# Graph layer kernel: finding each node's edges by samples, and the key sums taken as a column of the value product

## The chip, the cores and the metric

The kernel runs on one core of one Trainium2 chip. The metric is the device time of one execution, in microseconds (us), as the median of several runs. A profile is one further execution, recorded by the hardware profiler; its span is the time from its first to its last recorded instruction. The engines are PE (TensorE; its weight loads are listed apart, as PEld), DVE (VectorE), ACT (ScalarE), POOL (GpSimd) and SP, which issues most transfers.

## The reference

x has 1250 rows (nodes) of 1024 values. Everything below works on xn, the layer norm of x.

```
# graph part: 40,000 edges (src, dst, type), sorted by dst, 8 types
u = xn @ root + bias
for r in range(8):
    u += mean over the edges of type r into each node of xn[src] @ weight[r]
z = concat(u, xn) @ w_gate + b_gate
h = tanh(u) * z + xn * (1 - z)
# linear attention, 16 heads of 64
q, k = elu(xn@Wq)+1, elu(xn@Wk)+1;  v = xn@Wv;  g = sigmoid(xn@Wg + bg)
kv = k^T v (per head);  k_sum = sum of k over the nodes
out = (q*scale @ kv) / clip(q . k_sum) * g @ Wo
x = x + h + out
# gates, one step from a zero state
x = x + sigmoid(o) * tanh(sigmoid(i) * tanh(c)),  each of layernorm(x) @ W
```

## The kernel before, in words

**Dense products.** The 1250 nodes are ten tiles of 128 (the last has 98). PE computes 38 stages in a fixed order, each one weight matrix half (1024 by 512) against all ten tiles (stages `G_` and `Q_` use 12 units of 416 or 418 columns). One tile of one stage is a unit, numbered q from 0. Each product is made of three: high part by high part, and the two mixed terms, so a unit is 8 (k) times 3 = 24 matmuls. Units 0 to 159 are the `Y_` stages (xn by the eight relation weights), 160 to 179 `R_`, then `V_` (180 to 189 and 200 to 209), `K_` (190 to 199 and 210 to 219), `X_`, `G_`, `Q_`, `O_` and the gates. The order of every engine is written out by hand: each engine runs a loop over q and over k = 0 to 7, and small pieces of other work are put in at chosen (q, k).

**Weights.** A stage's weights come in four granules. SP loads a granule (`load_w`), ACT casts the high part (`hi_w`, L936) and DVE subtracts for the low part (`lo_w`, L1080) in units 1, 3, 5 and 7 of the stage before. `load_w` of granule n+2 waits until the low part of granule n is made, since the raw buffer has two places. SP's queue is in order: behind a waiting `load_w` stand the stores of finished units (`store_unit`, L536). ACT empties a PSUM tile into `res`, which has three places (`evict`, L961), and waits for the store of the unit three before (`free_res`). PE may start unit q when unit q-3 is evicted.

**Edge tables.** While the `Y_` stages run, the edges are sorted into per-node tables. DVE splits dst into tile and place (`edge_cells`, at the start, between `ln_x(1)` and `lo_w(4)`). In units 20 to 40 the edges per node and relation are counted: DVE writes one-hot tiles of 8 edges per partition (`count_step`, L1133) and PE multiplies them (L792), 40 steps of 8 matmuls. The counts give in-degrees, keys and reciprocals (`in_degrees`, unit 41), PE turns them into first positions (`run_starts`, unit 42), and POOL fetches for each node two rows of 64 edge codes (`read_run`, 20 indirect DMAs). DVE marks which codes belong to each node (`run_inside`, `run_keys`, `run_half`, units 43 to 46). In units 48 to 57, at each unit twice, DVE ranks a tile of nodes by degree (`rank_tile`, L1214 and L1215) and takes the 40 highest codes of a tile (`top_of`, L1225 and L1227). `tables` (units 59 and 61) makes row numbers and weights; POOL scatters the tables to memory (`send_rows`), SP loads them back (`load_edges`, L573, units 63 and 69: it waits for all ten scatters of a half). `columns_over` (DVE, unit 75) checks the table widths, `any_bad` (PE, unit 76, k = 2) sums the flags and `which_path` sets a flag `meta`: if it is 1, a slow general path loops over all edges.

**Sums.** From unit 82 POOL gathers rows of the `Y_` results (L1626) and DVE adds them up (`add_edges`, L1299), some 2.3 steps a unit, up to the `G_` stages.

**Keys and values.** Beside each `K_` unit PE adds one node tile to kv (`kv_tile`, k = 6 of the unit after): for each of four blocks of 128 columns one fp32 matmul of the key tile against the value tile (L821, PSUM bank `misc`) and one of the same key tile against two columns of ones (L824, bank `tp`), so 8 matmuls. The values come back from memory by `load_v`, one DMA a tile in pieces of 2048 bytes, into two places; the load for tile t waits until `kv_tile` t-2 is done.

Of the kernel before, what the change touches and what calls it, by code (L numbers as in the profile page):

```python
# [5 lines left out]
F32 = mybir.dt.float32  # L6
# [22 lines left out]
CB = 8  # L29
COUNTS = EC // CB  # L30
B = R * T
NOBODY = 1 << 20
# [4 lines left out]

RUN = 64
RUN_ROWS = E // RUN + 2
# [134 lines left out]
def build(nc, x, src, dst, edge_type, weight, root, bias, w_gate, b_gate, Wq, Wk, Wv, Wg, bg, Wo,  # L174
          W_iT, b_i, W_oT, b_o, W_cT, b_c, out):
    with ExitStack() as ctx:
# [19 lines left out]
        code_d = dram("code_d", [RUN_ROWS, RUN])  # L196
        key_d = dram("key_d", [2, T * 128])
# [23 lines left out]
        inv = put("inv", [128, B])  # L221
# [8 lines left out]
        ones2 = put("ones2", [128, 2])  # L230
# [19 lines left out]
        cells = at(e_at + 5120, "cells", [128, 2, EC], I32)  # L250
        bucket = at(e_at + 7680, "bucket", [128, EC])
        node = at(e_at + 8960, "node", [128, EC])
        b80 = at(e_at + 10240, "b80", [128, EC])
        code = at(e_at + 11520, "code", [128, EC])
        tmp = at(e_at + 12800, "tmp", [128, EC])
        falls = at(e_at + 14080, "falls", [128, EC])
        tail = at(e_at + 15360, "tail", [128, 1])
        assert e_at + 15392 <= end
        oh_node = at(wx_at, "oh_node", [128, 2, CB, 128], BF16)
        oh_bucket = at(wx_at + 4096, "oh_bucket", [128, 2, CB, B], BF16)  # L260
        before = at(wx_at + 6656, "before", [128, 128])
        assert wx_at + 7168 <= e_at


        nodes = at(M + 44448, "nodes", [128, T], I32)
        turned_key = at(M + 44512, "turned_key", [128, T])
        cnt = at(M + 44576, "cnt", [128, 2, T])
        deg = at(M + 44672, "deg", [128, T])
        key = at(M + 44736, "key", [128, 2, T])
        rank = at(M + 44832, "rank", [128, 2, T])  # L270
        slot = at(M + 44928, "slot", [128, 2, T], I32)
        first = at(M + 45024, "first", [128, T])
        run_row = at(M + 45088, "run_row", [128, 2, T], I32)
        run_off = at(M + 45184, "run_off", [128, T])
        most = at(M + 45248, "most", [128, T])
        assert M + 45312 <= end and M + 40960 + up(16 * COLS) + 32 * T <= M + 44448
        runs = at(M, "runs", [128, T, 2 * RUN])
        held = at(M + 5120, "held", [128, 2, T, 2 * RUN])
        dist = at(M + 15360, "dist", [128, T, 2 * RUN])
        inside = at(M + 20480, "inside", [128, T, 2 * RUN])  # L280
        made = at(M + 25600, "made", [128, T, 2 * RUN])
# [4 lines left out]
        p_at = M + 15360  # L286
        whole = at(p_at, "whole", [128, T, WIDE], I32)
        source = at(p_at + 1600, "source", [128, T, WIDE])
        relation = at(p_at + 3200, "relation", [128, T, WIDE])
        weigh = at(p_at + 4800, "weigh", [128, T, WIDE])  # L290
        part_w = at(p_at + 6400, "part_w", [128, T, WIDE])
        assert M + 33920 + 80 * ROW <= M + 40960


        vld = at(M, "vld", [128, 2, H])
        U = [at(M + 4096, "U0", [128, D]), at(M + 12288, "U1", [128, D])]
        kv = at(M + 8192, "kv", [128, PAIRS, 128])
        odd = at(M + 16384, "odd", [128, D])
        ring = at(M + 20480, "ring", [128, RING, D])
        edge = at(M + 40960, "edge", [128, 2, COLS, 2], I32)  # L300
        whose = at(M + 40960 + up(16 * COLS), "whose", [128, 2, T, 2], I32)
        assert M + 40960 + up(16 * COLS) + 32 * T <= end and RING * 4096 == 20480


        x_raw = at(M + 16384, "x_raw", [128, D], F32R)
        x_big = at(M + 20480, "x_big", [128, D], F32R)
        x_oh = at(M + 24576, "x_oh", [128, 128], F32R)
        x_edge = at(M + 25088, "x_edge", [128, 3], I32)
        x_part = at(M + 25120, "x_part", [128, 2], I32)
        x_sum = at(M + 25152, "x_sum", [128, 3])  # L310
        x_idx = at(M + 25184, "x_idx", [128, 3], I32)
        x_inv = at(M + 25216, "x_inv", [128, 1])
# [4 lines left out]
        o0 = at(M + 12288, "o0", [128, 4, N])  # L317
        o1 = at(M + 32288, "o1", [128, 2, 4, GROUPS[0][1]])
        assert M + 32288 + 32 * GROUPS[0][1] <= end
# [7 lines left out]
        lnb = at(M + 40960, "lnb", [128, 2, H])  # L327
# [8 lines left out]
        def turned_rows(w):  # L336
# [14 lines left out]
        edges_in, cells_made, edges_made, tail_made, codes_st, bg_in = (  # L351
            sem(n) for n in ("edges_in", "cells_made", "edges_made", "tail_made", "codes_st", "bg_in"))
        sum_const, cnt_oh, cnt_mm, inv_done, inv_st, deg_made, run_mm, run_made, runs_in = (
            sem(n) for n in ("sum_const", "cnt_oh", "cnt_mm", "inv_done", "inv_st", "deg_made", "run_mm", "run_made",
                             "runs_in"))
# [135 lines left out]
        def _(sp):  # L491
# [202 lines left out]
            for q in range(UNITS + 1):  # L694
# [13 lines left out]
                if q < UNITS:  # L708
# [10 lines left out]
                    if q == 43:  # L719
                        store_keys()  # L720
                    if q == 47:
                        load_keys()
# [1046 lines left out]
```

## Time and profile before

| what | value |
|---|---|
| median of 3 runs | 2356.18 us (2354.4 to 2358.92) |
| the profiled execution, its own time | 2352.61 us |
| its span | 2350.9 us |
| PE busy | 2241.8 us (95%) |
| PE weight loads busy | 1826.0 us (78%) |
| DVE busy | 1310.4 us (56%) |
| POOL busy | 710.6 us (30%) |
| ACT busy | 438.7 us (19%) |
| mean granted PE clock | 0.983 |

Busy time is the time in which an engine executes; where it is below the span, the views of waits and windows say where it stood still. Matmuls are pipelined, so one matmul's listed duration (0.39 us) is longer than the distance to the next.

### The profile page before, as it was taken

What the parts mean: (1) busy time and instruction counts of PE and PEld (TensorE: products, weight loads), DVE (VectorE), ACT (ScalarE), POOL (GpSimd) and SP (SyncE); (2) the same over time, 40 slices, a digit from 0 to 9 for tenths busy, and PEclk for the clock granted to TensorE, in tenths of its full rate; (3) what the DMA queues carried; (4) which work ended last, traced back from release to release, by engine and by line L of the source; (5) the groups of instructions that cost most, each with busy time, mean ns of one, the idle gap of its engine ahead of it and who ended that gap; (6) DMA issues with size and microseconds to landing.
All of it is one profiled execution on the core that took longest, in us unless ns stands there. A gap on an engine that the chain in (4) does not pass through costs nothing.

```text
span 2350.9 us, 26012 instructions
## 1 busy us (share of the span) xinstructions
PE 2241.8 (95%) x10294; PEld 1826.0 (78%) x10294; DVE 1310.4 (56%) x1695; ACT 438.7 (19%) x623; POOL 710.6 (30%) x586
## 2 busy tenths in 40 slices
PE   5999997399999999999999999999999799999999
PEld 4877775288888888888888888899887687887787
DVE  6446549931666666666645556765782347424233
ACT  2111111011111111110121210122231213322121
POOL 3200030041555556644534334561111254000000
PEclk9999998699999999999999999999999999999999
DMA  6442230143778888875767768883016865213112
GB/s 213 176 118 76 71 102 30 57 116 118 257 246 291 287 318 287 294 271 173 278 224 236 257 222 287 280 301 135 27 46 237 327 235 179 69 57 107 49 37 74
DMA packets 186039, 420.98 MB, mean 179 GB/s; under 512 B 34309, under 2 KB 41078, under 8 KB 185916
## 3 DMA queue, kind: packets, MB, share of 16 engines
q1 hardware_dynamic: 122716, 233.42, 28.9%
q0 software_dynamic: 63200, 185.89, 23.7%
q8 instruction: 81, 1.33, 0.2%
q14 instruction: 42, 0.34, 0.1%
HBM read 356.62 MB, written 103.70 MB: 196 GB/s over the span
## 4 chain that ended last, share of the span: by engine, by line
PE 81%; DVE 7%; issue 5%; DMA 4%; POOL 2%; SPq 0%; ACT 0%; POOLq 0%; DVEq 0%; ACTq 0%
PE acc L926 72%; PE acc L921 5%; DVE top_codes L1225 1%; DMA th_d<-tu 1%; DVE rank L1215 1%; DVE held L1227 1%; PE misc L821 1%; PE tp L779 1%; POOL o L1731 1%; DVE Wlo L1080 1%; DVE above L1214 1%; POOL runs L1606 1%; DMA uio<-u_d 1%; PE misc L792 1%; DMA tx<-xn_d 0%
## 5 line engine op out<-in xcount | busy, mean ns | idle before, releaser
L926 PE MATMUL acc<-Whi,aThi 128*128 128x512 f32 (+1 forms) x2720 | 1088.0, 400 | 71.5 <-DVE Wlo L1080 34.5
L926 PE MATMUL acc<-Whi,aTlo 128*128 128x512 f32 (+1 forms) x2720 | 1076.1, 396 | 0.0
L926 PE MATMUL acc<-Wlo,aThi 128*128 128x512 f32 (+1 forms) x2720 | 1074.0, 395 | 0.0
L926 PEld LDWEIGHTS acc<-Whi,aThi 128*128 128x128 f32 (+1 forms) x2720 | 507.8, 187 | 197.6 <-DVE Wlo L1080 37.4
L1626 POOL DMA_INDIRECT ring<-y_d,edge x390 | 480.1, 1231 | 515.0 <-DVE U L1299 173.4
L926 PEld LDWEIGHTS acc<-Whi,aTlo 128*128 128x128 f32 (+1 forms) x2720 | 507.3, 187 | 128.0
L926 PEld LDWEIGHTS acc<-Wlo,aThi 128*128 128x128 f32 (+1 forms) x2720 | 508.9, 187 | 122.8 <-issue 0.2
L1080 DVE TENSOR_TENSOR Wlo<-Wraw,Whi 128x1024 fp32r<-128x1024 f32 x149 | 186.4, 1253 | 266.4 <-ACT Whi L936 265.7
L961 ACT COPY res<-acc 128x512 f32<-128x512 f32 (+1 forms) x180 | 105.6, 587 | 931.4 <-PE acc L926 788.9
L1299 DVE SCALAR_TENSOR_TENSOR U<-ring,edge,U 128x1024 f32<-128x1024 f32 x180 | 230.3, 1279 | 33.1 <-DMA ring<-y_d,edge 32.8
L1299 DVE SCALAR_TENSOR_TENSOR odd<-ring,edge,odd 128x1024 f32<-128x1024 f32 x170 | 217.7, 1281 | 47.7 <-DMA ring<-y_d,edge 46.9
L936 ACT CAST Whi<-Wraw 128x1024 fp32r<-128x1024 f32 x149 | 155.4, 1047 | 197.2 <-PE acc L926 53.8
L1382 DVE TENSOR_TENSOR res<-acc,bias_sb 128x512 f32<-128x512 f32 x80 | 55.3, 692 | 187.4 <-PE acc L926 116.8
L921 PE MATMUL acc<-aThi,Whi 128*128 128x416 f32 (+1 forms) x384 | 142.3, 371 | 0.0
L921 PE MATMUL acc<-aTlo,Whi 128*128 128x416 f32 (+1 forms) x384 | 135.1, 352 | 0.0
L921 PE MATMUL acc<-aThi,Wlo 128*128 128x416 f32 (+1 forms) x384 | 134.8, 351 | 0.0
L1606 POOL DMA_INDIRECT runs<-code_d,run_row x20 | 21.1, 1055 | 182.6 <-DVE run_row L1171 176.8
L921 PEld LDWEIGHTS acc<-aThi,Whi 128*128 128x128 f32 x384 | 72.2, 188 | 4.7 <-issue 3.7
L921 PEld LDWEIGHTS acc<-aTlo,Whi 128*128 128x128 f32 x384 | 72.3, 188 | 4.4 <-issue 3.7
L1085 DVE TENSOR_TENSOR aTlo<-tp,aThi 128x1024 fp32r<-128x1024 f32 (+1 forms) x30 | 35.9, 1196 | 71.0 <-ACT aThi L940 71.0
L1361 DVE SCALAR_TENSOR_TENSOR res<-acc,res 128x512 f32<-128x512 f32 (+3 forms) x44 | 26.6, 604 | 85.3 <-ACT res L974 85.3
L921 PEld LDWEIGHTS acc<-aThi,Wlo 128*128 128x128 f32 x384 | 72.2, 188 | 0.7
(182 smaller groups left out, 1272.8 us busy)
## 6 DMA issues: line engine op xcount, KB each, us to landing
y_d<-res SPq DMA_DIRECT2D x144, 256.0 KB
Wraw<-in_L_gnn_weight SPq DMA_DIRECT2D x61, 512.0 KB, 4.8
Wraw<-in_L_gnn_w_gate SPq DMA_DIRECT2D x16, 512.0 KB, 6.4
ring<-y_d,edge POOLq DMA_INDIRECT x390, 6.5
xr<-in_x SPq DMA_DIRECT2D x9, 512.0 KB, 3.8
xn_d<-xnb SPq DMA_DIRECT2D x9, 512.0 KB, 3.0
xs_d<-xr SPq DMA_DIRECT2D x9, 512.0 KB, 3.8
ur_d<-res SPq DMA_DIRECT2D x18, 256.0 KB
```

Of the source, the lines that this page charges most:

```text
L779: tr = nc.tensor.transpose(tp[:, k // 4, (k % 4) * 128:(k % 4) * 128 + w], parts(k), ident[0:w, 0:w])
L921: mm = nc.tensor.matmul(to, a[:, s % 2, k, cols], b[:, k, c0:c0 + w], start=start, stop=stop)
L926: mm = nc.tensor.matmul(to, a[:, k, rows(i)], b[:, s % 2, k, :], start=start, stop=stop)
L936: nc.scalar.copy(granule(Whi, n), raw(n)).then_inc(w_hi, 1)
L961: nc.scalar.copy(res[0:width(i), q % 3, :], acc[0:width(i), q % 3, :]).then_inc(evac_a, 1)
L1080: nc.vector.tensor_tensor(granule(Wlo, n), raw(n), granule(Whi, n).bitcast(F32), ALU.subtract).then_inc(w_lo, 1)
L1085: nc.vector.tensor_tensor(aTlo[:, :, rows(t)], turned_rows(width(t)), aThi[:, :, rows(t)].bitcast(F32), ALU.subtract).then_inc(done, 1)
L1299: nc.vector.scalar_tensor_tensor(to, g, scale, to, ALU.mult, ALU.add).then_inc(u_acc, 1)
L1361: nc.vector.scalar_tensor_tensor(a, p, 0.0, a, ALU.max, ALU.add).then_inc(evac_v, 1)
L1382: nc.vector.tensor_tensor(to, p, bias_sb[0:w, n % 2, :], ALU.add).then_inc(evac_v, 1)
L1606: pool.indirect_dma_start(runs[:, t, i * RUN:(i + 1) * RUN], None, code_d, bass.IndirectOffsetOnAxis(ap=run_row[:, i, t:t + 1], axis=0), b ...
L1626: pool.indirect_dma_start(ring[:, j % RING, :], None, a, bass.IndirectOffsetOnAxis(ap=index, axis=0), bounds_check=top - 1, oob_is_err=Fal ...
```

## The change

1. **Counting goes.** `edge_cells`, the 40 `count_step`s (DVE and PE), `in_degrees` and `run_starts` are removed. `edge_codes` on POOL makes code = dst * 10000 + type * 1250 + src and a copy of every 64th code, the samples (625). They are stored to memory and read back to all 128 partitions (`load_samples`, SP, unit 21). DVE counts for each tile of nodes how many samples are below the node's first code (`count_below`, units 23 to 27), which gives the first row of 64 codes (`run_places`, unit 28).
2. **Marking moves and changes.** After the 20 indirect reads, DVE subtracts the node's code and compares with the half's limits (`run_codes`, `run_half`, `run_keys`, `hold_half`, units 36 to 39). The in-degrees are sums of these marks.
3. **Ranking and taking the highest codes are spread.** `top_of` and `rank_tile` run in two of every three units, once each, in units 41 to 72. Reciprocals of the counts per relation are made from the table itself (`tables_weights`, unit after `tables`). `tables` runs in units 58 and 73, `tables_weights` in 59 and 74, `load_edges` in 61 and 76, `columns_over` in 78, `any_bad` at unit 79 and `which_path` at unit 80.
4. **Keys and values.** The value tile is held as four blocks of 130 columns, 128 values and two ones, so that four matmuls of 130 columns give kv and the key sums; `load_v` writes it in pieces of 512 bytes.
5. The general path counts for itself; it does not run on these inputs unless a flag is set. The store of `inv` (unit 63) goes.

```diff
-                if k in (1, 5) and 0 <= 2 * q + k // 5 - 41 < COUNTS:
-                    count_step(2 * q + k // 5 - 41)
-                if q == 42 and k == 2:
-                    run_starts()
-                if q == 76 and k == 2:
+                if q == 79 and k == 2:
                     any_bad()
...
                 for m in range(4):
-                    nc.tensor.matmul(misc[:, m * 128:(m + 1) * 128], rows_k[:, m * 128:(m + 1) * 128],
-                                     vld[0:w, t % 2, m * 128:(m + 1) * 128], start=(t == 0 and m == 0),
-                                     stop=(t == T - 1), skip_group_check=True)
-                    mm = nc.tensor.matmul(tp[:, 0, 2 * m:2 * m + 2], rows_k[:, m * 128:(m + 1) * 128], ones2[0:w, :],
-                                          start=(t == 0 and m == 0), stop=(t == T - 1), skip_group_check=True)
+                    to = (misc[:, :] if m < 2 else tp[:, 0, :])[:, m % 2 * 130:m % 2 * 130 + 130]
+                    mm = nc.tensor.matmul(to, rows_k[:, m * 128:(m + 1) * 128], vld[0:w, t % 2, m, :],
+                                          start=(t == 0 and m % 2 == 0), stop=(t == T - 1), skip_group_check=True)
...
+            def load_samples():
+                sp.wait_ge(codes_st, 48)
+                for i in range(2):
+                    sp.wait_ge(xn_st[i], 16 * (T // 2))
+                    sp.wait_ge(xs_st[i], 16 * (T // 2))
+                sp.dma_start(sample_row[:, :], sample_d.rearrange("(o n) -> o n", o=1).to_broadcast([128, SAMPLES])
+                             ).then_inc(samples_in, 16)
...
+            def count_below(t):
+                if t == 0:
+                    dve.wait_ge(samples_in, 16)
+                    dve.wait_ge(const, 3)
+                chain(nc.vector.tensor_scalar(below[:, :], sample_row[:, :], node_code[:, t:t + 1], None, ALU.is_lt))
+                chain(nc.vector.tensor_reduce(below_n[:, t:t + 1], below[:, :], AX.X, ALU.add))
...
+            def run_half(h):
+                lowest, beyond = float(h * HALF_R * N), float((h + 1) * HALF_R * N)
+                chain(nc.vector.tensor_scalar(within[:, h, :, :], runs[:, :, :], lowest, None, ALU.is_ge))
+                chain(nc.vector.scalar_tensor_tensor(within[:, h, :, :], runs[:, :, :], beyond, within[:, h, :, :],
+                                                     ALU.is_lt, ALU.mult))
+                step.inc(nc.vector.tensor_reduce(bad[:, 1 + h:2 + h], within[:, h, :, 2 * RUN - 1], AX.X, ALU.max))
+                chain(nc.vector.tensor_reduce(cnt[:, h, :], within[:, h, :, :], AX.X, ALU.add))
...
+            def tables_weights(h):
+                for r in range(HALF_R):
+                    step.inc(nc.vector.scalar_tensor_tensor(of_r[:, r, :, :], relation[:, :, :], float(r),
+                                                            weigh[:, :, :], ALU.is_equal, ALU.mult))
+                step.wait(dve)
+                for r in range(HALF_R):
+                    step.inc(nc.vector.tensor_reduce(inv[:, r, :], of_r[:, r, :, :], AX.X, ALU.add))
...
+                for r in range(HALF_R):
+                    step.inc(nc.vector.tensor_tensor(of_r[:, r, :, :], of_r[:, r, :, :],
+                                                     inv[:, r, :].unsqueeze(2).to_broadcast([128, T, WIDE]), ALU.mult))
...
-                    if k in (1, 5) and 0 <= 2 * q + k // 5 - 40 < COUNTS:
-                        count_step(2 * q + k // 5 - 40)
...
-                    if 48 <= q < 48 + T and k in (1, 5):
-                        rank_tile((q - 48) // 5, 2 * ((q - 48) % 5) + k // 5)
...
-                    if 48 <= q < 48 + T and k in (2, 6):
-                        top_of((q - 48) // 5, 2 * ((q - 48) % 5) + k // 5)
...
+                    if k == 1 and 41 <= q < 71 and (q - 41) % 3 < 2:
+                        top_of((q - 41) // 15, 2 * ((q - 41) % 15 // 3) + (q - 41) % 3)
+                    if k == 5 and 43 <= q < 73 and (q - 43) % 3 < 2:
+                        rank_tile((q - 43) // 15, 2 * ((q - 43) % 15 // 3) + (q - 43) % 3)
+                    if q in (58, 73) and k == 1:
+                        ranks_whole((q - 58) // 15)
+                    if q in (58, 73) and k == 2:
+                        tables((q - 58) // 15)
+                    if q in (59, 74) and k == 1:
+                        tables_weights((q - 59) // 15)
+                    if q == 78 and k == 5:
+                        columns_over()
+                    if q == 80 and k == 2:
+                        which_path()
```

## Rows read from the trace of the kernel before

**Rows 1.** Page, costliest groups: count, busy and mean ns, idle before and its releaser

```profile
L1080 DVE TENSOR_TENSOR Wlo<-Wraw,Whi 128x1024 fp32r<-128x1024 f32 x149 | 186.4, 1253 | 266.4 <-ACT Whi L936 265.7
L961 ACT COPY res<-acc 128x512 f32<-128x512 f32 (+1 forms) x180 | 105.6, 587 | 931.4 <-PE acc L926 788.9
...
L936 ACT CAST Whi<-Wraw 128x1024 fp32r<-128x1024 f32 x149 | 155.4, 1047 | 197.2 <-PE acc L926 53.8
```

**Rows 2.** Windows: busy us (instructions) of PE, PEld, DVE, ACT, POOL; clock; DMA

```profile
345.00:463.00 118.00, 62.22 (x240) 47.69 (x240) 104.86 (x291) 9.94 (x15) 0.00 (x0) 0.78 0.16 53
463.00:551.00 88.00, 87.85 (x372) 70.60 (x373) 31.25 (x66) 15.93 (x23) 24.70 (x21) 0.98 0.38 115
551.00:1195.00 644.00, 644.00 (x2793) 515.76 (x2792) 388.19 (x340) 100.68 (x142) 336.60 (x274) 1.00 0.76 259
```

**Rows 3.** Waits of the whole span: us in total, times, longest

```profile
ACT res L961 <- DMA y_d<-res: 142.4, 10, 32.1
...
PE acc L926 <- DVE Wlo L1080: 34.5, 6, 20.8
...
PE acc L926 <- ACT res L961: 27.3, 2, 16.8
...
PE misc L792 <- DVE oh_bucket L1133: 3.3, 1, 3.3
```

**Rows 4.** Waits of SP's queue in the stretch 340 to 470 us

```profile
SPq L497 <- DVE Wlo L1080: 104.2, 4, 37.2
```

**Rows 5.** Timeline of DVE from 351 us: start, duration, instruction

```profile
351.19 0.89 DVE L1214 TENSOR_SCALAR above<-keyrow,key 128x1280 f32<-128x1280 f32 x1 [5.94 <-DMA keyrow<-key_d]
352.12 1.49 DVE L1215 TENSOR_REDUCE rank<-above 128x1 f32<-128x1280 f32 x1
...
356.84 0.89 DVE L1214 TENSOR_SCALAR above<-keyrow,key 128x1280 f32<-128x1280 f32 x1
```

**Rows 6.** Chain that ended last, in order of time: start, us, what

```profile
174.40 2.87 PE acc L926 x12
177.57 2.87 PE acc L926 x12
...
551.28 641.81 PE acc L926 x2772
```

**Rows 7.** Timeline of DVE and of PE before the first counting step

```profile
156.72 1.23 DVE L1080 TENSOR_TENSOR Wlo<-Wraw,Whi 128x1024 fp32r<-128x1024 f32 x1 [1.12 <-ACT Whi L936]
...
159.88 0.38 PE L792 MATMUL misc<-oh_bucket,oh_node 125*128 125x80 bf16 x3 [3.26 <-DVE oh_bucket L1133]
```

**Rows 8.** Timeline of PE's weight loads inside one kv_tile

```profile
1215.26 0.30 PEld L821 LDWEIGHTS misc<-vld,res 128*128 128x128 f32 x2
1215.48 0.30 PEld L824 LDWEIGHTS tp<-ones,res 128*128 128x128 f32 x2
1215.70 0.30 PEld L821 LDWEIGHTS misc<-vld,res 128*128 128x128 f32 x2
```

**Rows 9.** Timeline of DVE at the start of the kernel

```profile
21.93 0.32 DVE L1118 TENSOR_SCALAR cells<-raw_edges 125x320 int32<-125x320 int32 x1
...
23.93 1.35 DVE L1080 TENSOR_TENSOR Wlo<-wx,Whi 128x1024 fp32r<-128x1024 f32 x1
```

**Rows 10.** Timeline of DVE, POOL and SP around the first half's tables

```profile
468.73 0.36 DVE L1234 CAST whole<-top_codes 128x400 int32<-128x400 f32 x1
...
472.44 0.57 DVE L1249 SCALAR_TENSOR_TENSOR weigh<-relation,inv 128x400 f32<-128x400 f32 x1
...
478.31 1.02 POOL L1613 DMA_INDIRECT slot_d<-table,slot  x1 [151.87 <-DVEq L1259]
...
490.15 0.97 POOL L1613 DMA_INDIRECT slot_d<-table,slot  x1 [0.30 <-issue]
...
493.50 4.81 SPq L573 DMA_DIRECT2D edge<-slot_d  x10
```

**Rows 11.** DMA issues in 460 to 620 us: count, size, median us to landing

```profile
whose<-slot_d SPq DMA_DIRECT2D x2, 10.0 KB, 2.3
```

**Rows 12.** Tile vld: the DMA's time to landing, min, median, max

```profile
DMA to landing us min/median/max: 2.5/4.0/6.5
```

More of the change, by code:

```diff
@@ L271, in build @@
[L271 to L274, printed above, removed]
+        code = at(e_at + 5120, "code", [128, EC])
+        tmp = at(e_at + 6400, "tmp", [128, EC])
+        falls = at(e_at + 7680, "falls", [128, EC])
+        tail = at(e_at + 8960, "tail", [128, 1])
+        samples = at(e_at + 8992, "samples", [128, EC // RUN])
+        assert e_at + 9024 <= end
@@ L786, in turn_x @@
                 turn_rows(lambda k: xnb[0:width(t), t % 2, k * 128:(k + 1) * 128], width(t)).then_inc(x_turned, 1)
[L788 to L803 removed]
             def any_bad():
+                pe.wait_ge(const, 3)
                 pe.wait_ge(bad_made, 1)
@@ L884, in general_sums @@
                 with pe.If(general > 0):
+                    with pe.Fori(0, EC) as c:
+                        pe.wait_ge(xc_oh, c * 2 + 2)
+                        nc.tensor.matmul(agg[:, 0, 0:B], x_node[0:EP, :], x_bucket[0:EP, :], start=True, stop=True
+                                         ).then_inc(xc_mm, 1)
                     with pe.Fori(0, T * EC) as i:
@@ new lines, in run_places @@
+            def run_places():
+                chain(nc.vector.tensor_scalar(most[:, :], below_n[:, :], 1.0, 1.0, ALU.max, ALU.subtract))
+                nc.vector.tensor_copy(run_row[:, 0, :], most[:, :]).then_inc(run_made, 1)
+                nc.vector.tensor_copy(run_row[:, 1, :], below_n[:, :]).then_inc(run_made, 1)
+                dve.wait_ge(run_made, 2)
+                chain(nc.vector.tensor_scalar(run_row[:, 1, :], most[:, :], 1.0, None, ALU.add))
+                dve.sem_inc(run_made, 1)
@@ new lines, in across, with everywhere, run_codes @@
+            def across(a):
+                return a.unsqueeze(2).to_broadcast([128, T, 2 * RUN])
+            def everywhere(a):
+                return a.unsqueeze(1).to_broadcast([128, T, 2 * RUN])
+            def run_codes():
+                dve.wait_ge(runs_in, 16 * 2 * T)
+                chain(nc.vector.tensor_tensor(runs[:, :, :], runs[:, :, :], across(node_code[:, :]), ALU.subtract))
+            def run_half(h):
[5 more added lines that the diff above has]
+                chain(nc.vector.tensor_reduce(cnt[:, h, :], within[:, h, :, :], AX.X, ALU.add))
@@ L1193, in run_keys @@
[L1193 to L1207 removed]
+                dve.wait_ge(place_const, 2)
@@ new lines, in run_keys, with hold_half @@
+                chain(nc.vector.scalar_tensor_tensor(runs[:, :, :], runs[:, :, :], float(2 * RUN),
+                                                     everywhere(odd_places[:, :]), ALU.mult, ALU.add))
+            def hold_half(h):
+                chain(nc.vector.tensor_tensor(held[:, h, :, :], within[:, h, :, :], runs[:, :, :], ALU.mult))
+                chain(nc.vector.tensor_tensor(held[:, h, :, :], held[:, h, :, :], everywhere(next_places[:, :]),
+                                              ALU.subtract))
@@ L1545, in _ @@
-                    if q == 75 and k == 5:
+                    if q == 17 and k == 6:
+                        edge_order()
+                    if 23 <= q < 28 and k in (2, 6):
+                        count_below(2 * (q - 23) + k // 6)
+                    if q == 28 and k == 2:
+                        run_places()
+                    if q == 36 and k == 2:
+                        run_codes()
+                    if q in (36, 37) and k == 6:
+                        run_half(q - 36)
+                    if q == 38 and k == 2:
+                        run_keys()
@@ new lines, in _ @@
+                    if q in (38, 39) and k == 6:
+                        hold_half(q - 38)
+                    if k == 1 and 41 <= q < 71 and (q - 41) % 3 < 2:
[4 more added lines that the diff above has]
+                        ranks_whole((q - 58) // 15)
```

350 lines of the change are left out of this document (147 added, 203 removed).

## The prediction

> **What bounds the kernel now.** I read the page's groups first, then a table of windows, the waits, and the timelines of the places that the change touches. PE is the bound, but not everywhere. From 551.28 us on, 2772 matmuls take 641.81 us without a gap [rows 6]: 0.2315 us each, so a unit of 24 takes 5.56 us, and in the window 551 to 1195 PE stands still nowhere [rows 2]. A microsecond taken from DVE there is worth nothing. The stretch before it is different: in 345 to 463 us PE runs 240 matmuls in 118 us at a mean clock of 0.78, while DVE is busy 104.9 us of the 118 [rows 2].
>
> The waits say how DVE holds PE. One `rank_tile` and one `top_of` take 356.84 - 351.19 = 5.65 us [rows 5], and two of each are written into each unit, so 11.3 us of DVE work per 5.56 us of PE work. The low parts of the weights stand in the same queue and come late. SP's queue waits 104.2 us for them at `load_w` [rows 4], the stores behind it come late, ACT waits 142.4 us for stores before it may evict [rows 3], and PE waits 27.3 us for evictions and 34.5 us for the low parts [rows 3]. So this stretch is bound by DVE, through SP's queue.
>
> **The change, part by part.** The sum is made against the profiled execution, 2352.6 us (span 2350.9 and 1.7 around it), which is 3.6 us under the median of the runs.
>
> *The DVE-bound stretch.* From 345.0 to 551.28 us PE does 240 + 372 = 612 matmuls [rows 2]. At 0.2315 us they are 141.7 us, the stretch is 206.3 us: 64.6 us are lost, in waits and in the slow restarts behind them. After the change a period of three units (16.7 us) holds two `rank_tile`s and two `top_of`s, 11.3 us, and 1.2 subtractions of 1.25 us [rows 1], together 12.8 us or 77%. In the crowded spot around unit 59 (`tables`, two `top_of`s, a `rank_tile` or two and `tables_weights` between the subtractions of units 57 and 61) I add up: lateness 1.5 us before, then 4.1 (tables, as 468.73 to 472.44 [rows 10] and one added comparison), 2.4 (a `rank_tile`, 0.89 + 1.49 [rows 5]), 3.2 (a `top_of`, the rest of the 5.65), 8.9, 2.4 and 3.2, in all 25.7 us in DVE's queue before the subtraction of unit 61, where the four units leave 20.9 beside it; the subtraction of unit 61 is some 5 us late, that of 63 some 6.6, 67 is on time again. A granule is needed only in the next stage, two to ten units on, so PE does not wait for these. The 8.9 us of `tables_weights` are 11 passes over 400 columns at 0.5 to 0.58 us [rows 10], four reductions taken at the same price, and 0.9 for small ones (an estimate). Earlier, `count_below` is at most ten times 0.89 + 1.49 us [rows 5] in five units (27.8 us), and `run_codes` to `hold_half` are nine passes over 1280 columns and two reductions, at most 1.49 us each, about 17 us in the 22 us of units 36 to 39, where no subtraction is due after unit 37. The 20 indirect reads start in unit 28 and take 26 us at the 1.3 us pace of the scatters ((490.15 - 478.31)/9 [rows 10]); they are in by unit 33 and DVE asks at 36. I take the full 64.6 us; the lower bound is 50 (rival B and more of the kind).
>
> *Counting steps.* With one step in every 12 matmuls the pitch is 177.57 - 174.40 = 3.17 us [rows 6]; 12 matmuls alone are 2.78. A step costs 0.39, 40 cost 15.7 us. The first also made PE wait 3.26 us for its one-hot tile [rows 7]; without it PE waits for the subtraction that ends at 156.72 + 1.23 = 157.95, so 1.9 us earlier than 159.88. With less slow restart I take 2.9 us (1.5 to 4). `run_starts` is two narrow matmuls, 0.4 us.
>
> *New waits at the tables.* `tables` for the second half follows the subtraction of unit 71, `tables_weights` that of unit 73. A subtraction ends 2.9 us into its unit (evict 0.59, cast 1.05, subtract 1.25 behind PE's last matmul [rows 1]), so with 8.9 us the tables are ready 0.7 us into unit 75. The first scatter starts 0.9 later, ten take 490.15 - 478.31 + 0.97 = 12.8 us, SP goes on 493.50 - 491.12 = 2.4 us after that [rows 10]: start of unit 78. Its ten loads take 4.8 us, the last one 0.5 and 2.3 to land [rows 10, 11]: 2 us into unit 79. DVE needs 0.8 us for four small operations (an estimate), so the flag is made 2.8 us into unit 79, and `any_bad` stands on PE at k = 2, 1.4 us into it. PE waits 1.4 us there, where before it waited for nothing (range 0 to 5). In the meantime SP is held from unit 75 to 79, and store 75 goes out 5.3 us into unit 78; eviction 78, due at the start of unit 79, comes some 2 to 3 us late, and PE asks for it only at unit 81. For the first half the same count gives: tables ready 1 us into unit 61, SP free and store 60 out by the start of unit 65, landed 2.7 us into it, eviction 63 done 3.3 us into it, needed at 66: 2.2 us to spare. That is the thinnest cover of this change. If the scatters or the loads take longer by a half, 8 us, PE waits 6 us there.
>
> *Keys and values.* The weight loads of a `kv_tile` come in doubles (an fp32 matmul is shown twice), and follow at 0.22 us for wide and narrow alike [rows 8], 0.11 per pass: eight matmuls are 1.78 us. Four stay. If a pass is bound by its weight load, a tile costs 0.89; if the narrow passes were cheaper and the wide ones dearer than the mean by an eighth, 0.125 each, it costs 1.0. I take 0.94: saving 20 times 0.84 = 16.8 us (15.6 to 17.8). All of it is PE time in a stretch with no gap, so it counts in full. The V loads are in four pieces where one was; they land in 4.0 us (at most 6.5) [rows 12], and have two units with a `kv_tile`, 13 us. Six copies to SBUF instead of three happen between K stages and are covered by DVE's free time.
>
> The Trainium skill, TensorE: Matmul & The Clock Gate, Back-to-back issue gap, gives a sustained distance of about 81 ns per matmul of 128 columns, weight load included. By it the eight passes that stay would be 0.65 us, the saving 22.6 us and the sum 6 us lower. The trace does not agree: the same passes stand 0.11 us apart.
>
> *The start.* `edge_cells` sits in DVE's queue from 21.93 to 23.93 [rows 9], in front of subtractions that PE and SP's next loads wait for. 2.0 us go (0 to 3). The check of the order moves to unit 17, where DVE waits anyway. POOL's codes start before DVE is done and run beside it.
>
> The sum: 64.6 + 15.7 + 2.9 + 0.4 - 1.4 + 16.8 + 2.0 = 101.0 us, so 2251.6 us for the profiled execution, and 2255 us at the median of runs.
>
> **The rivals.** *B: the tables' transfers hold PE.* The mechanism above with longer scatters or loads: SP stands at `load_edges`, no store leaves, ACT can't evict. For it: this is just the chain that stopped PE before [rows 3, 4], and the cover is 2.2 us. Against it: at 463 to 551 us the same scatters and loads ran with an SP stop of the same kind, and PE lost next to nothing (87.85 of 88 us) [rows 2]. Two stops of 5 us with a slow restart each: 2268 us. *C: DVE stays late.* If the DVE steps between subtractions take a half longer than summed, 19 us per 16.7, each of ten periods loses 2.5 us, and with slow restarts half of the lost time stays, 32 us: 2287 us. Against it: the durations are measured. *D: the sums slip.* The K units are 0.84 us shorter, so the additions, tied to units, have 17 us less; the last could hold the first attention unit by 5 us: 2260. DVE is busy 388 of 644 us beside the sums [rows 2], which speaks against it. *E, on the other side: V loads come late.* If a load in 512-byte pieces takes so long that `kv_tile` waits, each of 20 tiles pays. The room is 13 us and the gain to be eaten 101/20 = 5 us a tile, so it decides from 18 us to landing, four and a half times the median of 4.0 [rows 12]; at 20 us the time is 2356 + 40 = 2396. *F: it doesn't do what it says:* if the samples placed a node's codes wrongly, a flag would send the kernel down the general path, 3200 passes with three gathers of at least a microsecond each [rows 10], 10,000 us more. An average node has 32 edges in 128 codes read, so I see no reason.
>
> **How the numbers follow.** Forecast 0.66 (2247 to 2263), B 0.15, C 0.06, D 0.05, a gain larger than summed (below 2247, all terms at their upper bound: 2246) 0.04, E and F 0.03, no change 0.01. The range goes from 2244 to 2275, which takes in B and D. What a measurement of this kernel can tell from no change is about 0.2%, 5 us. Faster 0.96, same 0.01, slower 0.03.
>
> **What the profile will show.** PE in units 41 to 75 without gaps, clock 1.00; no wait of SP at `load_w` over 10 us; pitch of 24 matmuls and a `kv_tile` 6.5 us where it was 7.33 (5.56 + 1.78); one wait of PE for `any_bad` near unit 79; PE's first products of unit 20 some 2 us earlier. Wrong if PE stands at units 64 to 68 or 79 to 81 for more than 3 us each, if a 130-column pass is slower than 0.13 us, or if DVE's queue is over 90% busy between units 41 and 75.

## The result

The changed kernel takes 2249.88 us at the median (2248.53 to 2253.43), the kernel before 2355.78 us on the same chip: a ratio of 0.9551 with an interval of 0.9534 to 0.9568. The forecast was 2255 us, in a range of 2244 to 2275. The profiled execution took 2253.43 us with a span of 2251.6 us; the span of before was 2350.9 us. Run once more, later, the ratio was 0.9561 (0.9548 to 0.9574) and the span of the profile 2249.5 us.

The windows of the changed kernel, columns as in [rows 2]:

```profile
290.00:380.00 90.00, 90.00 (x390) 71.83 (x390) 69.93 (x181) 15.08 (x22) 0.00 (x0) 1.00 0.24 81
380.00:470.00 90.00, 90.00 (x391) 72.40 (x390) 63.59 (x150) 15.98 (x24) 18.80 (x18) 1.00 0.30 95
490.00:1108.30 618.30, 618.30 (x2673) 495.08 (x2673) 384.54 (x337) 97.28 (x137) 334.11 (x274) 1.00 0.79 267
1110.00:1287.00 177.00, 177.00 (x844) 145.14 (x843) 104.41 (x103) 41.49 (x61) 80.69 (x67) 1.00 0.78 258
```

Read the two first lines against the first of [rows 2]. Where 240 matmuls took 118 us at a clock of 0.78, PE now does 781 in 180 us, 0.23 us each, at the full clock. DVE is busy 78% and then 71% of the time, where it was 89%. Its work is mostly spread and only a little smaller: over the whole execution it is busy 1250.4 us and was 1310.4. At the crowded spot around unit 59, from 360 to 405 us, it is still busy 42.5 of 45 us, and PE loses nothing there.

Waits of the changed kernel, lines cut from the list: first two in the whole span, then all but the last of SP's queue from 140 to 490 us (total, times, longest):

```profile
ACT res L960 <- DMA y_d<-res: 21.3, 3, 11.1
...
PE tp L795 <- DMA uio<-u_d: 13.0, 2, 9.3
```

```profile
SPq L534 <- ACT res L960: 206.3, 53, 5.9
SPq L495 <- DVE Wlo L1079: 58.0, 24, 7.4
SPq L582 <- DMA slot_d<-table,slot: 33.5, 2, 20.7
```

The chain that held PE has gone link by link. SP's wait for the low parts had single pieces of up to 37.2 us [rows 4] and has none over 7.4 us, in a longer stretch; ACT's wait for stores fell from 142.4 to 21.3 us; PE's waits for evictions, 27.3 us [rows 3], are not in the list any more.

The chain that ended last, in order of time:

```profile
483.19 625.14 PE acc L925 x2700
1109.22 5.55 PE acc L925 x24
1115.67 5.55 PE acc L925 x24
...
1287.28 106.96 PE acc L925 x462
1394.24 104.63 PE acc L920 x552
```

Its joints date the gain. The series of 2700 matmuls that ends at the first K unit begins at 483.19 us; in [rows 6] the same matmul stands 72 into the 2772, at 551.28 + 16.68 = 567.96 us. So 84.8 us are won by unit 79. The start of the x462 piece, behind the K stages, stood at 1389.64 us in the chain of before: 102.4 us are won there, so the K stages gave 17.6. From there on nothing more is won, and 99.3 us are left at the end: PE waits 13.0 us for `uio` where it waited 9.9. That last loss is scatter between executions: in the repeated profile of the same kernel the wait was 9.9 us again, and the span 101.4 us under that of before.

### The profile page after: what moved, and what is told of

It is laid out like the page before. It is cut to its first block, busy times and chain, and to the rows that moved or that the text cites. A ratio compares the mean times of both kernels' runs of the same rounds, so it can differ in the third digit from the quotient of the medians.

```text
span 2251.6 us, 25006 instructions
## 1 busy us (share of the span) xinstructions
PE 2200.0 (98%) x9810; PEld 1796.0 (80%) x9810; DVE 1250.4 (56%) x1647; ACT 439.0 (19%) x623; POOL 715.0 (32%) x589
## 4 chain that ended last, share of the span: by engine, by line
PE 68%; issue 5%; DMA 3%; POOL 1%; DVE 1%; SPq 1%; ACT 0%; POOLq 0%; DVEq 0%; ACTq 0%
PE acc L925 61%; PE acc L920 5%; DMA th_d<-tu 1%; POOL o L1745 1%; DMA uio<-u_d 1%; PE tp L795 1%; DMA tx<-xn_d 1%; PE tp L823 0%; PE misc L823 0%; POOL tu L1749 0%; DMA o<-g_d 0%; POOL slot_d L1626 0%; SPq L582 0%; DVE aTlo L1084 0%; DVE x_scale L1474 0%
## 5 line engine op out<-in xcount | busy, mean ns | idle before, releaser
L925 PE MATMUL acc<-Whi,aThi 128*128 128x512 f32 (+1 forms) x2720 | 1080.7, 397 | 15.9 <-DVE aTlo L1084 10.3
L1626 POOL DMA_INDIRECT slot_d<-table,slot x20 | 21.8, 1089 | 227.3 <-DVEq L1239 221.8
L1745 POOL TENSOR_TENSOR o<-o,rden 128x416 f32<-128x416 f32 (+1 forms) x24 | 24.7, 1029 | 143.3 <-DVE rden L1421 143.3
```

Source lines behind the costliest of these rows:

```text
L925: mm = nc.tensor.matmul(to, a[:, k, rows(i)], b[:, s % 2, k, :], start=start, stop=stop)
L1626: pool.indirect_dma_start(slot_d[h], bass.IndirectOffsetOnAxis(ap=slot[:, h, t:t + 1], axis=0), table[:, h, t, :], None).then_inc(sent[h], 16)
L1745: nc.gpsimd.tensor_tensor(o, o, rden[:, a % 2, 0:w], ALU.mult).then_inc(shared_out, 1)
```

## The experiments

Twelve kernels ran in three groups of four, each group on a chip of its own. "Against the changed kernel" means the median less 0.9551 times the median of the kernel before on that chip, or less that of a named run on the same chip.

**Ranking packed again.** Two rankings and two top steps per unit in units 48 to 57, all else as changed.

```diff
-                    if k == 1 and 41 <= q < 71 and (q - 41) % 3 < 2:
-                        top_of(...)
-                    if k == 5 and 43 <= q < 73 and (q - 43) % 3 < 2:
-                        rank_tile(...)
+                    if 48 <= q < 48 + T and k in (1, 5):
+                        rank_tile((q - 48) // 5, 2 * ((q - 48) % 5) + k // 5)
+                    if 48 <= q < 48 + T and k in (2, 6):
+                        top_of((q - 48) // 5, 2 * ((q - 48) % 5) + k // 5)
```

> The changed kernel with rank_tile and top_of packed as before, twice a unit in units 48 to 57, nothing else undone. My theory (DVE's queue, packed, held PE through late low parts, SP's queue and late stores): the 64.6 us come back, 2250 + 65 = 2315 us (2300 to 2325), PE idle of some 55 us and a granted clock under 0.85 in that stretch, SP's queue at load_w waiting some 100 us. Rival (the counting and its waits made the stretch slow, spreading is worth little): within 5 us of 2250.

2309.84 us, ratio 0.9775 (0.9757 to 0.9792): 54 us against the changed kernel. Windows from 380 to 440 us:

```profile
380.00:400.00 20.00, 11.37 (x36) 7.88 (x36) 18.59 (x58) 2.02 (x3) 0.00 (x0) 0.76 0.11 41
400.00:420.00 20.00, 2.92 (x6) 1.82 (x6) 18.79 (x49) 1.17 (x2) 0.00 (x0) 0.50 0.17 52
420.00:440.00 20.00, 14.97 (x54) 12.01 (x55) 18.86 (x52) 2.13 (x3) 0.00 (x0) 0.74 0.20 63
```

DVE is full, and PE does 6 matmuls in the middle one, where some 86 fit: the old bound is back with the old order alone, and so are its links: from 320 to 490 us SP's queue waits 91.0 us for low parts at `load_w`, ACT 102.5 us for stores, and PE 27.5 us for low parts and 15.9 for evictions. It costs a sixth less than the 64.6 us of before.

**Ranking spread and nothing else.** The kernel before, with one pair of steps per unit in units 48 to 67 and the tables, loads and checks moved behind them.

```diff
-                    if 48 <= q < 48 + T and k in (1, 5):
-                        rank_tile((q - 48) // 5, 2 * ((q - 48) % 5) + k // 5)
+                    if 48 <= q < 48 + 2 * T and k == 1:
+                        rank_tile((q - 48) // 10, (q - 48) % 10)
...
+                    if 48 <= q < 48 + 2 * T and k == 5:
+                        top_of((q - 48) // 10, (q - 48) % 10)
```

> The kernel before with its ranking spread out, one ranking and one top step in each of units 48 to 67 in place of two, its tables at units 69 and 71, the edges at 75 and 79, the checks at 82 to 85; nothing else of the change: the counting by samples and the products of key by value stay as they were. The theory (the stretch of units 48 to 57 was bound by DVE, and that alone is worth some 60 us) expects about 62 us less than the kernel before, a ratio of 0.974 (0.971 to 0.977), and PE busy throughout units 48 to 67. The rival (the gain needs the rest of the change, because the counting steps on DVE keep the engine too full when the ranking lies beside them) expects less than half of it, a ratio of 0.987 or more.

2314.35 us, ratio 0.9798 (0.9783 to 0.9813): 48 us less than the kernel before on that chip, where the theory said 62 and the rival at most 31: between the two, so that neither held as stated. Windows from 400 to 480 us:

```profile
400.00:420.00 20.00, 13.52 (x51) 10.55 (x50) 18.73 (x53) 2.88 (x5) 0.00 (x0) 0.83 0.38 127
420.00:440.00 20.00, 20.00 (x88) 16.20 (x88) 18.79 (x49) 3.24 (x6) 0.00 (x0) 1.00 0.15 53
440.00:460.00 20.00, 20.00 (x88) 16.09 (x87) 18.79 (x51) 3.54 (x5) 0.00 (x0) 1.00 0.15 53
460.00:480.00 20.00, 16.64 (x66) 12.63 (x65) 18.69 (x53) 2.69 (x4) 0.00 (x0) 0.91 0.37 124
```

My expectation left out a term. One pair a unit is 20 times 5.65 us [rows 5] and some eight subtractions of 1.25 [rows 1], 123 us, against 20 times 5.56 = 111 us of PE work. DVE was 94% busy and PE still waited for it, 9.8 us in two waits. In the two windows with these waits PE does 51 and 66 matmuls where 88 stand in the full ones; the 59 that are missing are 13.7 us, about the 14 by which the expectation was off. A stop of another kind at 505 to 513 us (see the last part) cost some 9 us more, against which the kernel before was itself 6.8 us slower on this chip. So one pair in each of 20 units is too dense for this DVE, and the 30 units of the change are enough. Most of the gain doesn't need the rest of the change; its part is that it makes the marks earlier, so that the ranking can start at unit 41.

**Old products of key by value.** Eight matmuls of 128 and 2 columns in place of four of 130.

```diff
-                    mm = nc.tensor.matmul(to, rows_k[...], vld[0:w, t % 2, m, :], ...)
+                    mm = nc.tensor.matmul(to[:, 0:128], rows_k[...], vld[0:w, t % 2, m, 0:128], ...)
+                    mm = nc.tensor.matmul(to[:, 128:130], rows_k[...], vld[0:w, t % 2, m, 128:130], ...)
```

> The changed kernel with each 130-column product split again into 128 columns and 2 columns, so eight matmuls a kv_tile. My theory (each pass costs its weight load, 0.11 us, however few columns): 20 x 0.89 = 17.7 us more, 2267.6 us, pitch of unit and kv_tile 7.33 us for 6.45. Rival (a two-column matmul is nearly free and the gain of this part came from elsewhere): at most 5 us more.

2273.51 us, ratio 0.9630 (0.9613 to 0.9646): 17.9 us against the changed kernel, as my theory had it (17.7), and the rival (at most 5) fell. The distance of the x24 pieces in the chain is 7.33 us again.

**Half the columns.** 66 of the 130 columns in 18 of the 20 tiles; half of each product is left out.

```diff
-                    mm = nc.tensor.matmul(to, rows_k[...], vld[0:w, t % 2, m, :], ...)
+                    c = 64 if t else 0
+                    mm = nc.tensor.matmul(to[:, c:130], rows_k[...], vld[0:w, t % 2, m, c:130], ...)
```

> The changed kernel with 66 instead of 130 moving columns in the products of 18 of the 20 kv_tiles: half of each key by value product is left out. My theory (a pass is bound by its weight load): same time, 2250 within 2 us, pitch 6.45 us as before. Rival (a pass is bound by its columns, 130 take 0.11 us): half of 0.89 us a tile goes, 18 x 0.44 = 8 us less, 2242 us, pitch 6.0 us.

2255.46 us, ratio 0.9546 (0.9529 to 0.9562): no difference. The chain of this run, and PE's weight loads in one tile of the changed kernel:

```profile
1123.04 5.60 PE acc L926 x24
1129.48 5.60 PE acc L926 x24
1135.92 5.60 PE acc L926 x24
```

```profile
1114.38 0.64 PEld L823 LDWEIGHTS misc<-vld,res 128*128 128x128 f32 x4
1114.95 0.52 PEld L823 LDWEIGHTS tp<-vld,res 128*128 128x128 f32 x4
1115.40 0.19 PEld L925 LDWEIGHTS acc<-Whi,aThi 128*128 128x128 f32 x1
```

6.44 us per unit with 66 columns, 6.45 with 130, so a tile costs 6.45 - 5.56 = 0.89 us with either. The first weight load of the tile stands at 1114.38, the second 0.23 us later, behind the 512-column product that is still running, the others 0.11 us apart (the rows put four in one), and the next product's at 1115.40. Together with the run before, where products of 2 columns stood just as far apart, this shows that the columns up to 130 are free. That it is the weight load which takes the 0.11 us, and not some other cost that every pass has, fits but is not shown: no run changed the weight loads and left the passes.

**The counting steps back on PE.** 40 times eight narrow matmuls, their result unused.

```diff
+            def idle_step():
+
+                for j in range(8):
+                    nc.tensor.matmul(misc[:, 0:B], spare[0:EP, :], spare[0:EP, 0:B], start=(j == 0), stop=(j == 7))
...
+                if k in (1, 5) and 0 <= 2 * q + k // 5 - 41 < 40:
+                    idle_step()
```

> The changed kernel with 40 times eight bf16 matmuls of 80 columns put back on PE alone, at the old places, from a constant tile: no one-hot tiles on DVE and nothing to wait for. My theory (the counting cost was PE's own time): 40 x 0.39 = 15.7 us more, 2265.6 us. Rival (it cost because PE waited for DVE's tiles, its own part hides behind weight loads): 0 to 4 us more.

2277.94 us, ratio 0.9649 (0.9633 to 0.9666): 22.3 us, 6.6 too many. The distance of the x12 pieces was 3.17 us, as in [rows 6], so the step itself costs 0.39 us. The waits of PE named the rest:

```profile
PE misc L808 <- issue: 6.1, 5, 1.8
PE acc L935 <- issue: 2.0, 4, 0.9
```

"issue" is standing still with nothing to wait for in the profile. All these waits lay between 217 and 230 us, while POOL issued the last of its 20 indirect reads (the last at 227.6 us) and just after. The other runs of that chip had a smaller stop at the same place. The last four runs come back to it.

**Loads of the edges too early.** `load_edges` in units 59 and 74, ahead of tables that are ready in units 61 and 75.

```diff
-                    if q == 61:
+                    if q == 59:
...
-                    if q == 76:
+                    if q == 74:
```

> The changed kernel with the two stores and loads of the edges' tables moved two units earlier, from units 61 and 76 to units 59 and 74, so that on SP's in-order queue they stand ahead of the tables that they need. The theory (SP's position counts: the tables are ready only in units 61 and 75, so SP would now stand still for more than a unit and the stores of rows that ACT needs come late) expects PE to wait some 8 us around unit 64, a slow restart behind it, and about 2 us near unit 79: some 12 us more than the changed kernel, a ratio to the kernel before of about 0.960. The rival (the stores have slack enough, SP's position in the queue is off the path) expects the changed kernel's own ratio, 0.955.

2268.59 us, ratio 0.9604 (0.9589 to 0.9619): 13 us above the two runs that follow, which were made on the same chip. Timelines of PE around 409 us and of ACT, and the waits of SP's queue in 300 to 500 us:

```profile
409.67 0.79 PE L925 MATMUL acc<-Whi,aThi 128*128 128x512 f32 x1 [7.84 <-ACT res L960]
```

```profile
409.04 0.59 ACT L960 COPY res<-acc 128x512 f32<-128x512 f32 x1 [22.25 <-DMA y_d<-res]
```

```profile
SPq L582 <- DMA slot_d<-table,slot: 31.8, 1, 31.8
```

This is rival B made real. SP stands 31.8 us, the store behind it is late, ACT's eviction waits 22.25 us and PE 7.84; from unit 78 to 80 PE waits another 1.58 us for an eviction and 1.69 for the flag. The rest of the 13 us is mostly the lower clock behind the long wait, 0.79 from 409 to 420 us. Two units of SP's order are worth 13 us here.

**Loads and checks later.** The loads in units 64 and 79, the check of the columns in 82, PE's flag in 84, the choice of the path in 85.

```diff
...
-                if q == 79 and k == 2:
+                if q == 84 and k == 2:
                     any_bad()
...
```

> The changed kernel with the loads of the edges three units later (units 64 and 79), the check of the columns at unit 82, PE's flag at 84 and the choice of path at 85. The theory (SP's stop at the tables now fits in the slack of the stores, and PE's wait for the flag is all that it costs) expects only the 0.5 to 1 us of PE's wait for the flag to change, the ratio of the changed kernel within 0.001, 0.955. The rival (SP's stop of some 20 us holds back the stores, and PE pays 3 to 5 us for it in small pieces that the profile does not name) expects 0.953 or less.

2255.65 us, ratio 0.9547 (0.9534 to 0.9560). PE's wait for the flag is gone from its list, SP's wait for the tables fell from 33.5 to 0.3 us, and the time is the same within the 3 us that the interval leaves: as placed, SP's stops cost nothing that can be seen beside that wait of 0.5 us.

**POOL's codes later.** POOL waits for the sixth low part of the weights before it makes the codes.

```diff
+            pool.wait_ge(w_lo, 6)
             edge_codes()
-            pool.wait_ge(w_lo, 5)
```

> The changed kernel with POOL's codes of the edges held back at the start until DVE has written the sixth low part of the weights and not the fifth, so that they no longer begin beside the second row tile's normalisation. The theory (POOL's work beside DVE's made DVE's operations longer, which cost the start some 0.8 us of its expected gain) expects PE's first product after its wait for the low part of the transposed rows near 41.4 us, not 42.07 us, and the three small operations of the normalisation back near 0.16 to 0.22 us from 0.32 to 0.36 us; 0.7 us lie below what the time can tell, so a ratio of 0.955. The rival (the load of the rows sets the start) expects that product at 42.1 us as before.

2255.16 us, ratio 0.9547 (0.9534 to 0.9560). Two operations of DVE in the changed kernel, then in this run:

```profile
21.48 1.07 DVE L1110 TENSOR_SCALAR xnb<-xr,stats 128x1024 f32<-128x1024 f32 x1
22.47 1.46 DVE L1079 TENSOR_TENSOR Wlo<-wx,Whi 128x1024 fp32r<-128x1024 f32 x1
```

```profile
20.93 0.81 DVE L1110 TENSOR_SCALAR xnb<-xr,stats 128x1024 f32<-128x1024 f32 x1
21.66 1.22 DVE L1079 TENSOR_TENSOR Wlo<-wx,Whi 128x1024 fp32r<-128x1024 f32 x1
```

Without POOL beside it DVE has its durations back, and PE's product after its wait stands at 40.33 us, where profiles with the unchanged start had it at 41.09 to 42.17. That theory holds; what it is worth, 0.8 to 1.8 us, is too little for the time to show.

**The stop of PE at 222 us.** The last four runs: the changed kernel again; POOL's reads in two groups; that with the counting steps; and the three small edits together.

```diff
                 for i in range(2):
+                    if i:
+                        pool.wait_ge(w_lo, 17)
                     for t in range(T):
                         read_run(i, t)
```

> The changed kernel as it is, beside the three that follow on the same chip. In the eight runs before this one PE stood still for 2 to 8 us near 222 us with nothing to wait for (only 'issue' in the waits), always while POOL issued the last five or so of its 20 indirect reads back to back (in the ranking-only kernel also in the last of its 20 scatters at 505 to 513 us); the profiles of the first chip, of the kernel before and of the changed one, show no such stop. The theory (the stop belongs to the long series of indirect transfers on this chip) expects 2 to 3 us of it here at 220 to 228 us and a ratio of 0.955. The rival (it belongs to the edits of the experiments) expects none.

> The changed kernel with POOL's 20 indirect reads in two groups of ten: before the second group POOL waits for the 17th low part of the weights, which DVE writes at 215.92 us in the profile after, some 4.6 us after the first ten are issued. The theory (a long series of indirect transfers without a pause is what starves PE) expects no 'issue' stop of PE between 210 and 235 us and 3 us less, a ratio of 0.9535 where the changed kernel has 0.955. The rival (it hangs on the number of reads or on the stretch of PE's program, not on the series) expects the stop at the same place of PE's program or behind the second ten, and no gain. DVE asks for the reads at 239 us, so the pause delays nothing.

> The run with the 40 counting steps put back on PE as work whose result is not used, now with the 20 reads in two groups as well. The theory (40 steps cost 40 times 0.39, 15.7 us, and the 22.3 us measured before held some 6.6 us of the 'issue' stop) expects 15.7 us more than the run with the split reads alone, and no stop near 220 us. The rival (the steps themselves cost 0.55 us each) expects some 22 us more again, without a stop.

> The changed kernel with three small edits together: the reads in two groups, POOL's codes of the edges held back by one low part of the weights, and the check of the columns and its flag four to five units later. The theory expects their sum, 3 us for the reads, 1.7 us at the start (PE's product after its wait for the low part of the transposed rows stood at 40.33 us in place of 42.07 us) and 0.5 us for the flag, 5 us in all: a ratio of 0.953 where the changed kernel has 0.955. The rival (time won at the start is given back before the end) expects no more than the split reads alone.

In the order given, with ratio and interval: 2251.71 us (0.9561, 0.9548 to 0.9574), 2251.80 us (0.9556, 0.9543 to 0.9569), 2265.34 us (0.9620, 0.9607 to 0.9633) and 2248.59 us (0.9550, 0.9537 to 0.9563). The changed kernel had no stop on this chip, so neither theory on the reads was put to the test, and the split had nothing to gain. The counting steps cost 13.5 us here; by the chains, where the x2700 piece starts at 498.03 and 483.96 us, 14.1; and counted from unit 20, which began 0.94 us earlier in the run with the steps, 15.0. The 6.6 us too many on the other chip belong to its stop: from the eviction of unit 27 to that of unit 36 the run with the steps took 69.3 us there and 57.0 here, so its stop cost some 12.3 us, and the three other runs of that chip lost 5.6 to 6.3 at this place. Whether the steps made the stop longer is open. The three edits together start the x2700 piece some 2.2 us earlier than the repeated run (its x2580 piece, 120 matmuls on, at 508.19 us, against 482.65 + 27.8) and have the lowest median; 1.0 of the 2.2 us is PE's wait for the flag in the repeated run. The intervals overlap, so no gain is shown.

## Why the prediction was right

The sum was 101.0 us and the forecast 2255 us, 5 above the median measured; the spans differ by 99.3 and, with the repeated profile, by 101.4. The 105.9 us between the medians are more because the profiled execution of before lay 3.2 us under its median and that of after 3.6 above.

*The DVE-bound stretch*, 64.6 us: right. Taken directly, from the eviction of unit 42 to that of unit 81, the kernel before needs 281.5 us and the changed one 217.6, in which is the wait of 0.5 for the flag: 64.4 us. By what is left over it comes to the same: of the 84.8 us won by unit 79, 1.2 are the start, 3.5 the end of the wait in unit 20, 15.2 the other 39 steps (at 0.39) and 0.4 `run_starts`, and 0.5 are lost at the flag; 65.0 are left. The experiments split it: 54 us are the order of the ranking. The other 10 I can only argue: in before the marking passes and the load of the keys stood right in front of the ranking, which in the packed run starts at 313.2 us and not at 351.2 [rows 5]. My addition of DVE's lateness held: the subtraction of unit 61 starts at 387.19 us, 4.7 us late (5 predicted).

*Counting steps*, 15.7 and 2.9: the step is right by its distance in the chain, and 13.5 to 15.0 us in sum when put back on a chip without the stop; the difference is in part the scatter of the start. The first wait gave 3.5 us.

*Waits at the tables*, 1.4: right in mechanism, 0.9 too large. The timelines of POOL and SP and of PE at the second half's tables:

```profile
459.95 0.97 POOL L1626 DMA_INDIRECT slot_d<-table,slot  x1 [64.05 <-DVEq L1239]
...
474.86 4.59 SPq L582 DMA_DIRECT2D edge<-slot_d  x10
...
482.84 0.35 PE L808 MATMUL misc<-bad,ones_all 128*128 128x2 f32 x2 [0.51 <-DVE bad L1248]
```

The tables were ready 0.4 us into unit 75 (0.7 predicted), SP was free 0.5 us before unit 78 (at its start), and the flag was made 1.8 us into unit 79 (2.8). At the first half eviction 63 had 3.4 us to spare where I gave it 2.2. So rival B stayed away, by a cover that was as thin as said: 11 us more of SP's time, in the run with the early loads, cost 13.

*Keys and values*, 16.8: 17.6 measured, near the upper end of 15.6 to 17.8. The step that was off is the choice of 0.94 us per tile; it is 0.89, the case that I had called "bound by its weight load", of which the runs show that narrow and wide passes cost the same. I had hedged toward dearer wide passes, which half the columns showed not to exist. The 81 ns that the Trainium skill, TensorE: Matmul & The Clock Gate, Back-to-back issue gap, gives for a matmul of 128 columns stayed too low for these passes: they stand 0.11 us apart in all runs. By that figure the time, and not the sum of the gains, would have come out some 6 us lower.

*The start*, 2.0: the weakest term, and one that a single pair of profiles can't size. In the first pair 1.0 to 1.2 us are won, in the repeated profile 2.0; over the ten profiles with the changed start PE's product behind its wait stands at 41.09 to 42.17 us, over the two with the old start at 43.11 and 43.44. "POOL's codes start before DVE is done and run beside it" stood in my text without a price. It had one: DVE's long operations beside them took a fifth to a third longer, some small ones up to twice as long. The next load of weights behind them moved by 0.8 us (32.94 for 33.70), not by the 2.0 removed.

Rivals C, D, E and F left no trace: C, as DVE is busy 144.5 of the 194 us from 269 to 463 us, its lateness stayed what was added up, and no low part held PE after unit 20; D, as the x462 and x552 pieces behind the K units take 211.6 us together, and 211.7 in before; E, as PE is busy 177.00 of 177.00 us in the window of the K units; F, as the time alone shows that the fast path was taken.

## What to carry to other kernels

Where two engines share a stretch, compare their work per period before asking which instruction is slow: 11.3 us against 5.56 told where the gain lay, the matmuls that were missing there told its size, and 123 against 111 us told why a half-way spread leaves 14 of it. Count every tenant of the period, the small periodic ones too. On an in-order queue that also carries stores, a load may stand late at no cost, but two units too early it cost 13 us; its slack is worked out from the landing of what it waits for to the eviction that needs the store behind it.

## What the hardware showed that was not expected

*A stop that came on two chips only.* On two chips PE stood still without a releaser, in the profiles of all eight kernels that ran there; the six other profiles (four on a third chip, and those of the kernel before and the changed one) show none. In seven of the eight it lay around 222 us, as POOL issued the last of 20 back-to-back indirect reads and up to 3.5 us after. In the run with only the ranking spread the reads come later, and so did the stop, at 327 to 331 us; a second one came in the last of its 20 scatters in a row (505 to 513 us). Windows of the half-column run, then of the changed kernel:

```profile
220.00:224.00 4.00, 2.87 (x12) 2.06 (x11) 0.32 (x1) 1.53 (x2) 2.99 (x3) 1.00 0.21 67
224.00:228.00 4.00, 2.03 (x5) 1.30 (x5) 0.90 (x1) 0.08 (x1) 1.65 (x1) 0.66 0.54 157
228.00:232.00 4.00, 4.00 (x10) 3.08 (x10) 0.00 (x0) 0.50 (x1) 0.00 (x0) 0.50 0.21 79
```

```profile
220.00:224.00 4.00, 4.00 (x19) 3.26 (x18) 0.00 (x0) 0.50 (x1) 3.09 (x4) 1.00 0.37 121
```

A window also counts a matmul that reaches into it; by their starts, it is 24 matmuls in these 12 us where the changed kernel has 52. The 28 missing are 6.5 us at 0.2315, 3.1 of them standing still and the rest at the lower clock behind it (0.66 and 0.50 in the rows). The kernel before was 6 to 7 us slower at the median on these chips too; no profile of it was kept there. That the supply of PE's instructions or its transfers are held up by the indirect ones is a guess; what these chips differ in, whether one chip shows it at all times, and whether groups of ten would avoid it, stays open.

*POOL slows DVE, but not every operation.* Beside POOL's passes DVE's subtraction took 1.46 and not 1.22 us, its normalisation 1.07 and not 0.81, and of the one-column operations with two inputs one took 0.36 and not 0.22, another 0.32 and not 0.16. Between these the one-column operations with one input kept their time; in the changed kernel, in order:

```profile
20.54 0.36 DVE L1094 SCALAR_TENSOR_TENSOR stats<-stats 128x1 f32<-128x1 f32 x1
20.94 0.15 DVE L1095 TENSOR_SCALAR stats<-stats 128x1 f32<-128x1 f32 x1
21.13 0.32 DVE L1096 TENSOR_TENSOR stats<-stats 128x1 f32<-128x1 f32 x1
```

The Trainium skill, SBUF — State Buffer, Who interferes with whom, says just this: an instruction of DVE with two inputs in SBUF contends with GpSimd's reads, one with a single input does so only in its faster modes. By that the trace agrees in which operations grew; the normalisation has one input and does 1024 columns in 0.81 us where the subtraction needs 1.22. The same section calls the ports that the two share an exclusive lock, by which the later one would wait until the other is done; the subtraction grew by 0.24 us beside a pass of POOL of over 1 us, so DVE's side does not show a full wait. POOL's passes grew as well: beside the two subtractions that follow, a conversion of 320 columns took 1.32 us, and 0.45 in the run with the codes later. How the two share the wait stays open.
